# Adding the partial sums of the two middle token stages in DRAM

## The reference, cut to what matters

```python
# condition: a 2048 x 2048 weight, quantized against a 32-entry codebook, with a LoRA correction
normalized = (weight + lora_delta).reshape(O, I // 128, 128) / exp(scale_log)
quantized  = cb[searchsorted(thresholds, normalized, side='left')]
w_eff      = (quantized * scale).reshape(O, I) + lora_delta
h          = x @ w_eff.T                                   # x: 32 x 128 tokens of 2048
# feed-forward: base weight, a 16-wide adapter mixed by an 8-way router
result = h @ W_base.T + b_base
ax     = h @ A_w.T
probs  = softmax(h @ router_w.T)
result = result + mixed(ax, cores, probs) @ B_w.T * 2
out    = x + result
```

## Time and profile before

| | |
|---|---|
| median of 3 runs | 2323.36 us (2320.93 to 2325.94) |
| the profiled execution | 2321.67 us |
| its span, first to last instruction | 2319.9 us |
| TensorE busy | 2239.5 us (97%) |
| VectorE busy | 1959.8 us (84%) |
| ScalarE busy | 1497.4 us (65%) |
| GpSimd busy | 1393.2 us (60%) |
| all DMA | 459.63 MB, mean 198 GB/s |

### The profile page before, as it was taken

How to read it: one execution, slowest core, us unless ns; L and a number is a source line. 1 busy time by engine, 2 the same in 40 slices (tenths; PEclk the granted TensorE clock), 3 DMA queues, 4 the chain that set the end, 5 groups by cost and what they waited for, 6 DMA issues and landing times.

```text
span 2319.9 us, 31904 instructions
## 1 busy us (share of the span) xinstructions
PE 2239.5 (97%) x11610; PEld 2019.9 (87%) x11610; DVE 1959.8 (84%) x2501; ACT 1497.4 (65%) x1962; POOL 1393.2 (60%) x902
## 2 busy tenths in 40 slices
PE   3989899999999999999999999999999999999999
PEld 2445479999999988899999989899999999999998
DVE  8999988889987977999987987999996776776776
ACT  7999978989887765666764865666663664122121
POOL 6888836669875545988775635988872132233331
PEclk9999999999999999999999999999999999999999
DMA  6788854444334334666664434666656665656554
GB/s 209 276 283 284 315 193 172 163 165 153 133 128 146 118 108 170 245 228 246 256 230 147 118 109 152 236 247 243 248 215 199 187 193 187 237 192 228 195 217 155
DMA packets 133234, 459.63 MB, mean 198 GB/s; under 512 B 14114, under 2 KB 66914, under 8 KB 96354
## 3 DMA queue, kind: packets, MB, share of 16 engines
q1 hardware_dynamic: 133076, 457.59, 56.5%
HBM read 306.41 MB, written 151.13 MB: 197 GB/s over the span
## 4 chain that ended last, share of the span: by engine, by line
PE 84%; ACT 6%; DVE 5%; POOL 2%; DMA 1%; issue 1%; SPq 0%; POOLq 0%; DVEq 0%; ACTq 0%
PE m L1233 6%; PE m L1232 6%; PE m L1234 6%; PE m L1184 5%; PE m L1186 5%; PE m L1185 5%; PE m L1339 4%; PE m L1341 4%; PE m L1340 4%; PE m L1289 4%; ACT mk L1454 4%; PE m L1291 4%; PE m L1290 4%; PE m L1125 3%; PE m L1300 3%; PE m L1299 3%
## 5 line engine op out<-in xcount | busy, mean ns | idle before, releaser
L1706 DVE SCALAR_TENSOR_TENSOR acc<-mk,dj,acc 128x1024 f32<-128x1024 uint8 x736 | 944.1, 1283 | 67.0 <-ACT mk L1454 48.2
L1454 ACT ACTIVATE mk<-wr,bj 128x1024 uint8<-128x1024 f32 x736 | 811.3, 1140 | 1.7 <-DVE acc L1706 1.4
L2019 POOL TENSOR_TENSOR pp<-pp,tm 128x1024 f32<-128x1024 f32 x184 | 455.5, 2476 | 22.9 <-POOL tm L2005 1.5
L2005 POOL TENSOR_SCALAR tm<-mp,dj 128x1024 f32<-128x1024 uint8 x192 | 228.5, 1190 | 204.5 <-ACT mp L1460 197.5
L1804 DVE TENSOR_TENSOR kl<-kw,kh 128x416 fp32r<-128x416 f32 (+3 forms) x310 | 239.8, 782 | 83.8 <-ACT kh L1489 82.4
L1489 ACT ACTIVATE kh<-kw 128x416 fp32r<-128x416 f32 (+3 forms) x310 | 169.3, 548 | 180.0 <-DMA kw<-in_wb 91.4
L1232 PE MATMUL m<-gh,xh 128*128 128x384 f32 (+2 forms) x800 | 280.8, 351 | 1.8 <-DVE part L1766 1.8
L1233 PE MATMUL m<-gl,xh 128*128 128x384 f32 (+2 forms) x800 | 280.9, 351 | 0.0
L1234 PE MATMUL m<-gh,xl 128*128 128x384 f32 (+2 forms) x800 | 279.8, 350 | 0.0
L1460 ACT ACTIVATE mp<-wr,bj 128x1024 uint8<-128x1024 f32 x224 | 255.3, 1140 | 13.7 <-POOL wr L1985 13.7
L1766 DVE TENSOR_TENSOR part<-m,part 128x512 f32<-128x512 f32 (+4 forms) x362 | 218.8, 613 | 37.8 <-PE m L1234 16.2
(11 more groups left out here) (249 smaller groups left out, 5163.1 us busy)
## 6 DMA issues: line engine op xcount, KB each, us to landing
part<-part SPq DMA_DIRECT2D x191, 1036.0 KB, 4.8
rows<-in_wb SPq DMA_DIRECT2D x61, 1036.0 KB, 4.8
out<-part SPq DMA_DIRECT2D x31, 1024.0 KB, 4.7
kw<-in_ws SPq DMA_DIRECT2D x128, 208.0 KB, 2.7
xw<-in_x SPq DMA_DIRECT2D x96, 256.0 KB, 3.3
kw<-in_wb SPq DMA_DIRECT2D x92, 192.0 KB, 2.4
wr<-in_w SPq DMA_DIRECT2D x32, 512.0 KB, 5.9
dl<-delta SPq DMA_DIRECT2D x30, 512.0 KB, 5.1
```

The source lines that it names most:

```text
L1454: e.activation(R.mk[m % NM], w, ACT.Identity, bias=R.bj[:, j:j + 1], scale=GROW).then_inc(S["mk"], 1)
L1706: e.scalar_tensor_tensor(R.acc, R.mk[m % NM], R.dj[:, j:j + 1], R.acc, ALU.mult, ALU.add).then_inc(S["ac"], 1)
L2019: e.tensor_tensor(R.pp, first, R.tm[scaled_level(q, i)], ALU.add).then_inc(S["pp"], 1)
```

## The change

1. **Sums in DRAM.** In stages 1 and 2 `part[t]` is no longer loaded. Each unit's bank is copied to the SBUF tile (only the second and third product of a target still add there), and POOL issues one DMA for each token that adds the tile to `part[t]` in DRAM (`add_part`, rows split in two pieces of 1036 columns). The DMA of the first token of a pair stands behind unit 10 (unit 6 in plain pairs), that of the second behind unit 1 of the next pair. Token 31's goes in four quarters at slots 1, 4, 7 and 10 of the next weights. SyncE's part loads and stores of these stages are gone.
2. **Eviction.** ACT copies the rests and chunks 0 to 2 (`mul_copied`), DVE the products and chunks 3 and 4 (`mul_evicted`).
3. **Low parts.** `spread_low` goes from POOL to DVE, and from units 1 to 4 of pair 0 to units 4, 5 and 6 of pair 0 and 2 of pair 1; `x_low` of the second token of pairs 1 to 15 goes from POOL to DVE, placed three units later in mixed pairs (one later in pair 0). The last step of `spread` goes from unit 2 to unit 3, `late_normalised` (POOL) from unit 8 to unit 2 of pair 1.
4. **Ring and background.** Slots 0 to 5, 10 and 11 of stages 2 and 3 are guests in freed buffers (x tiles, sums, `dl`), so that two loads of condition weight, on SyncE, wait for slots 5 and 11 of stage 2. `WAIT_LEVELS` goes from 6 to 8.

```diff
-GUEST = {4: 2, 5: 0}
-GUEST_LAST = {2: 0, 3: 1, 10: 0, 11: 1}
+GUESTS = {1: {4: "x2", 5: "x0"},
+          2: {0: "las", 1: "x0", 2: "x1", 3: "x2", 4: "sh", 5: "x3", 10: "las", 11: "sh"},
+          3: {0: "las", 1: "x0", 2: "x1", 3: "x2", 4: "sl", 5: "dl", 10: "sl", 11: "dl"}}
+SPREAD_AT, SPREAD_HIGH_AT = (0, 1, 3), (1, 2, 3, 4)
+SPREAD_LOW, SPREAD_LOW_AT = (2, 0, 1, 3), ((0, 4), (0, 5), (0, 6), (1, 2))
+LAST_AT = (1, 4, 7, 10)
-WAIT_LEVELS, END_LEVELS, WAIT_SLOTS = 6, 11, 4
+WAIT_LEVELS, END_LEVELS, WAIT_SLOTS = 8, 11, 4
...
             if at == 4:
                 yield ("x_split", g, 2 * p + 3)
-                yield ("more", g, p)
...
-            if at == 7:
+            if at == (10 if mixed(p) else 8):
                 yield ("x_low", g, 2 * p + 3)
...
+        if at == (10 if mixed(p) else 6):
+            yield ("half_stored", g, p)
+        if p and at == 1:
+            yield ("pair_stored", g, p - 1)
...
+def by_scalar(u):
+    return u[1] == "rest" or u[1] == "chunk" and u[3] in ACT_CHUNKS
+def x_low_on_vector(g, t):
+    return g in MIXED and t % 2 == 1 and t > 1
...
 # sync_program, weight
         elif s < RING or first_at_home(g, s):
             p = HOME[r]
-            e.wait_ge(S[f"po{p}"], 16 * (g * PER_SLOT[p] + (g == LAST and p == (NT - 1) % 3)))
+            if g == 1:
+                e.wait_ge(S[f"po{p}"], 16 * PER_SLOT[p])
+            else:
+                e.wait_ge(S[f"pa{p}"], stored_round(g - 1, NT - 1 - (NT - 1 - p) % 3))
...
-    def load_part(g, t):
-        if t < 3:
-            e.wait_ge(S["used"], NS * (g - 1) + RELEASED[t])
-        else:
-            e.wait_ge(S[f"po{t % 3}"], slot_round(g, t - 3))
-        e.dma_start(R.part[t % 3], part[t]).then_inc(S[f"pi{t % 3}"], 16)
...
 # scalar_program
+    def mul_copied(g, k):
+        p, kind, u, i = UNITS_OF[g][k]
+        t = 2 * p + u
+        part, bank = R.part[t % 3], (*R.m, R.pd)[unit_bank(UNITS_OF[g][k])]
+        if t >= 3 and k == token_units(g, t, True)[0]:
+            e.wait_ge(S[f"pa{t % 3}"], stored_round(g, t - 3))
+        e.wait_ge(S["mc"], multiplied(g, k))
+        ...
+        e.activation(to, of, ACT.Copy).then_inc(S["ea"], 1)
...
 # vector_program, mul_added becomes mul_evicted
-        if k == first_unit(g, t, 0):
-            e.wait_ge(S[f"pi{t % 3}"], slot_round(g - 1, t))
+        if t >= 3 and k == token_units(g, t, False)[0]:
+            e.wait_ge(S[f"pa{t % 3}"], stored_round(g, t - 3))
         e.wait_ge(S["mc"], multiplied(g, k))
         if kind == "chunk":
...
+            e.tensor_copy(part[:, cols(at[1])], bank[:, 0:width(at[1])]).then_inc(S["ed"], 1)
+            return
...
+        before = target_before(g, k)
+        if before is None:
+            e.tensor_copy(to, of).then_inc(S["ed"], 1)
+            return
+        wait_unit_evicted(e, S, g, before)
         e.tensor_tensor(to, of, to, ALU.add).then_inc(S["ed"], 1)
...
 # gpsimd_program
+    def add_part(g, t, i=0):
+        wait_unit_evicted(e, S, g, token_units(g, t, True)[-1])
+        wait_unit_evicted(e, S, g, token_units(g, t, False)[-1])
+        if g == 1:
+            e.wait_ge(S[f"po{t % 3}"], 16 * PER_SLOT[t % 3])
+        else:
+            e.wait_ge(S[f"pa{t % 3}"], stored_round(g - 1, t))
+        if t == NT - 1:
+            at = slice(DX // 4 * i, DX // 4 * (i + 1))
+            e.dma_start(part[t][:, at], R.part[t % 3][:, at], accum_op=ALU.add).then_inc(S[f"pa{t % 3}"], 16)
+        else:
+            e.dma_start(part[t], R.part[t % 3], accum_op=ALU.add, max_dma_last_dim=4 * HX).then_inc(S[f"pa{t % 3}"], 16)
...
-        elif what == "x_split" and at[0] and at[1] < 2 or what == "x_low":
+        elif what == "x_split" and at[0] and at[1] < 2 or what == "x_low" and not x_low_on_vector(*at):
             split_x(*at)
-        elif what == "spread_low":
-            spread_low(*at)
+        elif what == "half_stored":
+            add_part(at[0], 2 * at[1])
+        elif what == "pair_stored":
+            add_part(at[0], 2 * at[1] + 1)
+        elif what == "last_stored":
+            add_part(at[0], NT - 1, at[1])
```

218 lines of the change are left out of this document (119 added, 99 removed), and 2 rows, old and new, of the table COMPUTE.

## The result

The changed kernel takes 2331.41 us (median of 6 runs, 2327.35 to 2333.29), the kernel before 2323.48 beside it: ratio 1.0033, 95% interval 1.0022 to 1.0043. It is **slower by 0.33%** where 0.37% faster was forecast. The profiled execution is 2331.97 us with a span of 2330.2, 10.3 above before's span.

What follows compares the result with a forecast made beforehand. TensorE, busy 97% of the span, was taken as the bound; 9.0 us of waits returned plus 0.5 at the fifth place less 1.0 for new waits gave −8.5 us: 2314.9 us, 0.37% faster, range 2308 to 2318.7, chance 0.58.

Steps and rivals of the forecast that it cites:

- the four places: TensorE's waits in each token stage, three at its start and one in pair 2: 9.8 us for both stages, 9.0 returning.
- The loads of GpSimd and ScalarE: Busy time forecast for a token stretch of 338.7 us: GpSimd 293.5 us (87%), ScalarE 262 us (77%).
- ScalarE's term: Token stages: ScalarE gains rests and chunks, 46.7 us; masks up to 1.1 us later, covered by bank slack of some 9 us.
- Less 1.0 us for new waits: Deduction for new TensorE waits in the 28 mixed pairs of both token stages, 1.0 us in all.
- stage 3's first slots: Start of stage 3's weights, where loads and stores change places: no change, within ±2 us.
- The start of stage 2's weights: Fifth TensorE place, 1.1 us, an eviction behind two low parts of weights on VectorE: gain 0 to 1.1, taken as 0.5.
- By latency ... both ends fit: Token tiles: additions landing in 9.0 us, at most 16.5, fit 15.0 us before VectorE waits and 17.9 before TensorE does.
- Evictions that wait for a DMA: Listed sign that the forecast is wrong: evictions waiting for a DMA; no size given.
- the low part of x on VectorE: Token stages: 15 low parts at 1.25 us each move to VectorE, adding 18.8 us per stage.
- rival B: GpSimd becomes the bound through issues stretched to 3.3 us each; 2346 us, from 2328 up; chance 0.14.
- A (waits exchanged, 2318.7 to 2328): Rival: token-stage waits only exchanged, through late masks and evictions queued on VectorE and ScalarE; 2322.5 us; chance 0.20.
- C's, that additions fill the DMA engines: Rival: additions too slow for the DMA engines, deciding from 1.67 times a load and store; about 2427 us; chance 0.08.

Runs made afterwards that it cites:

- A: Kernel before with only the low parts of the sums (`spread_low`) moved to VectorE, in new order and places, and `WAIT_LEVELS` 8; 2316.38 us, ratio 0.9970.
- E: Changed kernel with ScalarE's masks ahead of everything else of a unit in stages 1 and 2; 2323.93 us, ratio 1.0006.
- F: Changed kernel with stage 2's four additions of token 31 cut to one row of 128 each (measuring only); 2326.15 us, ratio 1.0015.
- I: E with every addition in DRAM cut to one row of 128 (measuring only); 2310.86 us, ratio 0.9952.
- J: B with every addition in DRAM cut to one row of 128 (measuring only); 2320.63 us, ratio 0.9990.
- B: Changed kernel with all evictions of stages 1 and 2 on VectorE and all low parts of x on GpSimd; 2344.68 us, ratio 1.0092.
- H: E and F together: masks first, and stage 2's additions of token 31 with one row each (measuring only); 2321.57 us, ratio 0.9995.
- K: E with VectorE's low part of each odd token of x three units later; 2337.54 us, ratio 1.0065.
- G: Changed kernel with stage 2's whole additions of token 31 held until slots 3 to 6 of stage 3 are multiplied; 2329.2 us, ratio 1.0027.

## Why the prediction was wrong

**Right.** That the four places were VectorE's `spread` beside GpSimd's low parts, and would go: they are gone in the changed kernel, and three of four in A, which alone gives 7.1 us (6.4 against the runs beside it). The loads of GpSimd and ScalarE within 9 us, the issue (1.2 us, taken as 1.3), the engine time of an addition (two passes), its landing (9.4 us at the median, 16.6 at most; taken as 9.0 and 16.5).

**Failed first: ScalarE's term.** The text had the coupling ("no longer runs ahead with the masks, so VectorE may get one up to 1.1 us later") and took as its cover the bank slack of a rest, six units. But the late mask does not hold up the rest's bank. It holds up what lies behind it in VectorE's queue, product 1's copy, whose bank is wanted after four. And the lateness was no 1.1 us: up to 4.3, as two rests and a load of x stand in line. "Less 1.0 us for new waits" measured 10.2, not all of it by masks. E, which changes only ScalarE's order, gives 7.5 us.

**Failed second: stage 3's first slots, "taken as 0, within ±2 us".** They cost 6.3 us. The places of loads in the ring were thought of; the additions of token 31 that share their first microseconds were not, and neither was TensorE's clock, which fell to 0.53 there (2.5 us). F gives 5.3 us. The start of stage 2's weights, "0 to 1.1 us, taken as 0.5", is off as well: 1.6 us at `lasl` in place of 1.1 before. In I and J this place is 0.3 and 0.4 us; no run isolates its cause.

**Failed third: "By latency ... both ends fit".** 15.0 us of cover against 9.0 of landing allowed for the issue, but not for its wait. Between last eviction and landing lies the issue's own wait in GpSimd's queue, 9.2 us ahead of 1505.61 in E. "Evictions that wait for a DMA" was among the text's own signs of being wrong, and it came. VectorE waited 4.7 us for additions in the changed kernel, 12.2 in E and 15.8 in B; B's pair with J puts the traffic, with what it adds to the issues, at 24 us, I's with H at 10.7.

**Mis-sized: the low part of x on VectorE, 1.25 us.** As a mean this was right (1.27), and as a load nearly (20.2 us for 18.8). What it hid is the spread: the median is 0.92, and twice it is over 3.7, once ahead of the largest place (1.88 us). VectorE's 12 us above the forecast come from other low parts, `wl` most of all. The stretching of the earlier trace rows was in the text, for the issues (rival B), where it didn't come: the longest issue is 1.68 us. The moved low part, itself an operation with two inputs, was not asked the same question. The Trainium skill's page "SBUF — State Buffer", section "Who interferes with whom", tells of VectorE and GpSimd excluding one another at their shared port; K's 4.40 us beside 2.85 fit that, and the issue's 1.2 us fit its inference that leaves such issues alone. What holds a low part that starts ahead of GpSimd's operation, during the issue (999.33 against 999.70 in the changed kernel), stays open.

**The rivals.** A (waits exchanged, 2318.7 to 2328) had the mechanism and too small a size; it named the late masks and ScalarE's loads of x, and was given 0.20. The measured time lies above A's range and in B's (from 2328 up), by luck and not by B's mechanism, which fell: no issue was stretched to 3.3 us, and GpSimd is not full. C's, that additions fill the DMA engines, fell as well (share 0.67); they cost by coming late, not by filling. The three failed terms lie on the same side; the sum had 1.0 us for them together.

**The account** (medians): −7.1 for G's low parts; the rest of the change +15.0. Of these, masks cost 7.5 and stage 3's start 5.3 by themselves, 9.8 together (H). That leaves 5.2 us, for which late additions and stretched low parts on VectorE are the causes seen; their shares were not measured one by one. Not tried: additions with GpSimd's queue kept free ahead of each, and the ring's new places by themselves.

## To carry to other kernels

When work moves to an engine with spare time, ask what that engine makes for others and what now stands ahead of it: an eviction waits for TensorE, and everything behind it in the queue inherits that wait. The cover to check is that of the last thing in the chain (who is behind the late operand in the consumer's queue, and when is that wanted), not that of the moved piece. For a transfer that frees a buffer, count eviction, queue ahead of the issue, issue and landing; and an issue placed "at slot 4" in a program comes when its own waits allow, not with the slot.

## What was not expected of the hardware

An accumulating DMA of 1036 KB issued by GpSimd keeps it for 1.18 to 1.68 us (0.32 us for SyncE's plain load) and lands in 9.4 us; with one row it takes 0.79 and 2.2 us. Loads on another queue land up to 7.9 us after their issue beside four quarter-size ones (4.3 us at most when these have one row). A VectorE subtraction of 128x512, 0.68 us by itself, took 3.7 to 4.8 us where it started during such an issue with a GpSimd addition of 128x1024 (2.8 to 2.85 us) right behind; away from issues it took 2.96 us at most. One of 128x1024, 1.21 us by itself, took 8.79. And TensorE's granted clock fell from 0.99 to 0.53 where TensorE had stood 1.5 us and then stood 2.6 us more (changed kernel, stage 3's start); with 4.5 us of standing in pieces of at most 1.9 us (G) it stayed at 1.00.
